# Four of eighteen V products per tile on GpSimd in the channel stage of a four-layer transformer kernel

## The chip, the cores and the metric

The kernel runs on one core of one Trainium2 chip, in one launch. The metric is the device time in microseconds (us); lower is better. The engines are named PE (TensorE), DVE (VectorE), ACT (ScalarE), POOL (GpSimd) and SP (SyncE, which here only issues transfers). Times inside a run are counted from the start of the profiled span. Lnnn is a line of the kernel before, in the text and in its profile.

## The reference, cut to what matters

The batch of 4 sequences of 512 tokens with 128 features goes through four layers, each an attention and a feed-forward part with a layer norm behind each. All is fp32. The change touches the attention of the last layer, which attends between the 64 channels of a head within one token, not between tokens:

```python
# x: (4, 512, 128); H = 16 heads, C = 64 channels
Q = (x @ Wq + bq).reshape(b, s, H, C) / sqrt(C)
K = (x @ Wk + bk).reshape(b, s, H, C)
V = (x @ Wv + bv).reshape(b, s, H, C)
scores = einsum('bshq,bshk->bshqk', Q, K)      # 64 x 64 for every token and head
scores = where(k > q, -inf, scores)
attn = einsum('bshqk,bshk->bshq', softmax(scores), V)
x = layernorm(x + attn.reshape(b, s, H * C) @ Wo + bo)
```

It also moves two weight matrices of earlier layers, the output projections `L1_attn_Wo` and `L2_attn_W_proj` (1024 x 128 each, 512 KB), in SBUF.

## The kernel before, in words

A loop runs over the 4 items of the batch. In each item the stages follow one another: attention and feed-forward of layers 0, 1 and 2, then the channel attention of layer 3 ("the channel stage"), then the feed-forward of layer 3 (eight experts). Each engine has its own instruction list, written out in order by a Python function per engine, and the engines wait on one another through semaphores (`wait_ge`). Nothing is reordered: an instruction that waits holds up all behind it on its engine.

The channel stage takes the 512 tokens of an item as NT = 4 tiles of 128 tokens (one token per partition). For a tile the scores of all 16 heads, causal part only, are cut into NC = 18 chunks of at most 1536 columns: chunks 0 to 5 for the upper half of the queries, 6 to 17 for the lower half without its first 8 queries. A chunk has one to five pieces (blocks of neighbouring keys with the same queries); each piece is one instruction on DVE or POOL. Chunks 0 to 3 have two pieces each, chunks 6 to 14 one piece of 1536 columns. A chunk passes these steps:

- POOL, line L1321: product q*k into one of the five buffers D3 (chunk n uses buffer n mod 5). It waits until the chunk five before has been weighed and its denominator summed.
- DVE, L1366 (`subtract`): subtracts an upper bound of the scores, which `maxima` (L1352 to L1354) has put in PSUM from two scans over the keys (`scan_keys`, L1339).
- ACT, L1297: exponential in place.
- DVE, L1380 (`weigh`): multiplies with V, read from PSUM (`psV`), into one of the two buffers W3.
- PE, L1201 (`sum_chunk`): sums over the keys by transposing matmuls that accumulate in PSUM, once for the denominator (psD, from D3) and once for the numerator (psA, from W3). "den(c)" and "num(c)" are these for chunk c of a tile. The numerator of a chunk is issued one chunk later than its denominator.

The scores of the first 8 queries of the lower half ("own" scores) are made apart, by 128 ACT instructions per tile (L1287), nine or ten behind the exponential of each of the chunks 1 to 14, into the single buffer EA. When all are done, PE sums them (L1210, `sum_own`) in four parts for the denominator at chunks 15 and 16, DVE multiplies them with V (L1386) at chunks 16 and 17, and PE sums them for the numerator at chunk 17 and at chunk 0 of the next tile. Only then may ACT write EA again, at chunk 1 of the next tile.

DVE's list per chunk c is: what is due at c (`maxima` at 0 and 14, `scan_keys` at 12, `finish` at 3 and 8, residual at 7), then subtract(c + 2), then weigh(c). PE projects Q and K of the next tile at chunks 8 to 11 (`fill_qk`, L1172 and L1173: two matmuls and two for the bias), behind num(c - 1), and ACT moves each result to SBUF at chunks 9 to 12 (L1269, L1273), behind the exponential of that chunk. V of a tile is projected in two halves, at chunk 17 of the tile before and at chunk 3.

Weights lie in SBUF for the whole launch, except those of layer 0's feed-forward: they are loaded again by SP at each item's end (L1452), since the channel stage's buffers reach over their place (`LENT` columns behind the shared `arena`). SP then waits for the last norm, writes the output (L1455), and waits for both.

Of the kernel before, what the change touches and what calls it, by code (L numbers as in the profile page):

```python
# [9 lines left out]
ALU = mybir.AluOpType  # L10
# [3 lines left out]
P = 128  # L14
# [43 lines left out]
def transformer(nc, inp, out, last_stage=8):  # L58
    ctx = ExitStack()
    with ctx:  # L60
# [21 lines left out]
        wq1 = sb("wq1", NH * HD)  # L82
        wk1 = sb("wk1", NKV * P)
        wv1 = sb("wv1", NKV * HD)
        wo1 = sb("wo1", NPAIR * P)
        wfc = sb("wfc", HID)
        wpj = sb("wpj", NM * P)
        wa2 = sb("wa2", 3 * NH * HD)
        wo2 = sb("wo2", NPAIR * P)
        ba2 = sb("ba2", 3 * NPAIR)  # L90
        bp2 = sb("bp2", 1)
        bo2 = sb("bo2", 1)
# [21 lines left out]
        stream = [sb(f"stream{j}", SLOT) for j in range(NSLOT)]  # L114


        AR, LENT = 24576, 2 * HID + 2 * NM * HID + NM * P
        arena = sb("arena", AR + LENT)
        top = [AR]

# [8 lines left out]
        w2_0 = take(HID)  # L129
        wh_0 = [take(NM * HID) for _ in range(2)]  # L130
        w3_0 = take(NM * P)

        top[0] = 0

# [51 lines left out]
        D3 = [take(CHUNK) for _ in range(5)]  # L186
        W3 = [take(CHUNK) for _ in range(2)]
        EA = take(HD * NH * OWN)

        top[0] = 0  # L190
        lat = take(HID)
# [16 lines left out]
        def tiles(a, n=P):  # L208
# [9 lines left out]
        ffn0_weights += [(tiles(w, HID), inp[f"L0_ffn_{name}_w"].rearrange("(k p) n -> p k n", p=P))  # L218
                         for w, name in zip(wh_0, ("h1", "h2"))]
        ffn0_weights += [(tiles(w3_0), inp["L0_ffn_w3_w"].rearrange("(k p) n -> p k n", p=P))]  # L220

        consts = sem("consts")
        small_in = sem("small_in")
# [10 lines left out]
        with nc.Block() as block:  # L234
# [15 lines left out]
            @block.scalar  # L250
            def _(act):
                def load(dst, src):
                    act.dma_start(dst, src).then_inc(weights_in, 16)
                    n_w[0] += 16

                load(wqk0[:], inp["L0_attn_QK"])
                load(wvo0[:], inp["L0_attn_VO"])
                for dst, src in ffn0_weights:
                    load(dst, src)
                for j, name in enumerate(("w1", "w2", "h1", "h2")):  # L260
                    load(s_0[:, j * NM:(j + 1) * NM], inp[f"L0_ffn_{name}_s"])
                load(s_0[:, 4 * NM:4 * NM + 1], inp["L0_ffn_w3_s"])
                load(wq1[:], inp["L1_attn_Wq"])
                for half in range(2):
                    load(tiles(wk1[:])[:, :, half * HD:(half + 1) * HD],
                         inp["L1_attn_Wk"].rearrange("d (k c) -> d k c", c=HD))
                load(wv1[:], inp["L1_attn_Wv"])
                load(tiles(wo1[:]), inp["L1_attn_Wo"].rearrange("(k p) n -> p k n", p=P))
                load(wa2[:], inp["L2_attn_W_attn"])
                load(tiles(wo2[:]), inp["L2_attn_W_proj"].rearrange("(k p) n -> p k n", p=P))  # L270
# [137 lines left out]
        def arrived(j):  # L408
# [7 lines left out]
        pr_ = {k: sem(f"prune_{k}") for k in ("s0", "sc", "ff", "bias", "w", "step")}  # L416
        c3 = {k: sem(f"c3_{k}") for k in (
            "d", "e", "w", "den", "num", "attn", "proj", "qk", "qk_sb", "v", "kh", "prod", "chain", "rT",
            "own", "own_den", "own_w", "own_num", "q_ps", "neg")}

        def x_ready(eng, stage):

# [712 lines left out]
        OWN_W = {NC - 2: (0, 1), NC - 1: (2, 3)}  # L1135
        OWN_NUM = {NC - 1: (0, 1), 0: (2, 3)}

        def of_own(o):
            return EA[:, o * PART * NH * OWN:(o + 1) * PART * NH * OWN]

# [73 lines left out]
        def channel_pe(pe):  # L1214
            s = c3
            x_ready(pe, 6)
            for j in range(4):
                fill_qk(pe, 0, j)
            fill_v(pe, 0, 0)
            pe.wait_ge(s["kh"], 2)  # L1220
            idle_work(6, 24)
            for n in range(NALL + 1):
                tt, c = n // NC, n % NC
                if n < NALL:
                    if tt > 0 and c == 0:
                        pe.wait_ge(s["attn"], 2 * tt - 1)
                    if tt > 0 and c == EARLY:
                        pe.wait_ge(s["attn"], 2 * tt)
                    pe.wait_ge(s["e"], n + 1)
                    sum_chunk(psD, D3[n % 5], n).then_inc(s["den"], 1)  # L1230
                if n > 0:
                    pe.wait_ge(s["w"], n)
                    sum_chunk(psA, W3[(n - 1) % 2], n - 1).then_inc(s["num"], 1)
                if n < NALL:
                    for o in OWN_DEN.get(c, ()):
                        pe.wait_ge(s["own"], (tt + 1) * len(own))
                        sum_own(psD, o).then_inc(s["own_den"], 1)
                if n >= NC - 1:
                    of = tt if c == NC - 1 else tt - 1
                    for o in OWN_NUM.get(c, ()):  # L1240
                        pe.wait_ge(s["own_w"], of * PARTS + o + 1)
                        sum_own(psA, o).then_inc(s["own_num"], 1)
                if n == NALL:
                    break
                if c == V1_AT:
                    if tt > 0:
                        pe.wait_ge(s["w"], tt * NC)
                        pe.wait_ge(s["own_w"], tt * PARTS)
                    fill_v(pe, tt, 1)
                if c == PROJ_AT and tt > 0:  # L1250
                    pe.wait_ge(s["d"], tt * NC + EARLY)
                    project_out(pe, tt - 1)
                if c in FILL_AT and tt + 1 < NT:
                    fill_qk(pe, tt + 1, FILL_AT[c])
                if c == V0_AT and tt + 1 < NT:
                    pe.wait_ge(s["w"], tt * NC + LATE)
# [49 lines left out]

        def channel_pool(pool):
            s = c3
            for n in range(NALL):
                tt, c = n // NC, n % NC  # L1310
                ch = chunks[c]
                if c == 0:
                    pool.wait_ge(s["qk_sb"], 4 * tt + 4)
                if n >= 5:
                    pool.wait_ge(s["w"], n - 4)
                    pool.wait_ge(s["den"], n - 4)
                q_half = Q3[tt % 2][:, ch.half * HB_:(ch.half + 1) * HB_]
                for piece in ch.pieces:
                    k, nk, w, at = piece
                    q = queries_on(q_half, ch, piece).rearrange("p k (q h) -> p k q h", h=NH)  # L1320
                    last = nc.gpsimd.tensor_tensor(of_piece(D3[n % 5], piece), q, keys_on(K3[tt % 2], k, nk, w), ALU.mult)  # L1321
                last.then_inc(s["prod"], 1)

        def channel_dve(dve):
            s = c3
# [42 lines left out]

            def weigh(n):
                tt, c = n // NC, n % NC  # L1370
                dve.wait_ge(s["e"], n + 1)
                if c == 0:
                    dve.wait_ge(s["v"], 2 * tt + 1)
                if c == LATE:
                    dve.wait_ge(s["v"], 2 * tt + 2)
                if n >= 2:
                    dve.wait_ge(s["num"], n - 1)
                for piece in chunks[c].pieces:
                    k, nk, w, at = piece
                    last = nc.vector.tensor_tensor(of_piece(W3[n % 2], piece), of_piece(D3[n % 5], piece),  # L1380
                                                   keys_on(psV, k, nk, w), ALU.mult)
                last.then_inc(s["w"], 1)
# [59 lines left out]
        with nc.Fori(0, BATCH) as b:  # L1442
            with nc.Block() as block:
                @block.sync
                def _(sp):
# [2 lines left out]
                    moe_sp(sp, ("L2_ffn_W1", "L2_ffn_W2", "L2_ffn_W3"), 0)  # L1448
                    moe_sp(sp, ("L3_ffn_W1", "L3_ffn_W2"), NE)
                    sp.wait_ge(nrm["xT"], 7)  # L1450
                    for dst, src in ffn0_weights:
                        sp.dma_start(dst, src).then_inc(w0_in, 16)  # L1452
                    sp.wait_ge(nrm["x"], 8 * NT)
                    y = out[bass.ds(b, 1)].rearrange("o (i p) d -> p (o i) d", p=P)
                    sp.dma_start(y, tiles(x[:])).then_inc(y_out, 16)  # L1455
                    sp.wait_ge(y_out, 16)
                    sp.wait_ge(w0_in, 16 * len(ffn0_weights))

                @block.tensor
                def _(pe):  # L1460
# [121 lines left out]
```

## Time and profile before

| what | us |
|---|---|
| median of 3 runs (lowest, highest) | 3764.69 (3761.5, 3766.67) |
| the profiled execution's own time | 3765.0 |
| its span | 3763.4 |
| busy in the span: PE, DVE | 3193.0, 2395.7 |
| busy in the span: ACT, POOL | 1966.7, 1330.0 |
| first item's channel stage, first instruction to the norm's xT | 497 to 890 |

The busy times are over the whole span, and the stages have different limits, so they are to be read stage by stage. "Idle before" an instruction is the time its engine stood still ahead of it, and the arrow names what ended it. Rows of the timeline merge instructions of one line that follow one another: start, time from the first's start to the last's end, engine, line, operation, and the number after x. Since instructions of an engine overlap a little at their ends, the cost of one in a row of several is the distance of two starts.

### The profile page before, as it was taken

What the parts mean: (1) busy time and instruction counts of PE and PEld (TensorE: products, weight loads), DVE (VectorE), ACT (ScalarE), POOL (GpSimd) and SP (SyncE); (2) the same over time, 40 slices, a digit from 0 to 9 for tenths busy, and PEclk for the clock granted to TensorE, in tenths of its full rate; (3) what the DMA queues carried; (4) which work ended last, traced back from release to release, by engine and by line L of the source; (5) the groups of instructions that cost most, each with busy time, mean ns of one, the idle gap of its engine ahead of it and who ended that gap; (6) DMA issues with size and microseconds to landing.
All of it is one profiled execution on the core that took longest, in us unless ns stands there. A gap on an engine that the chain in (4) does not pass through costs nothing. (4 is left out here: it accounts for less than half of the span.)

```text
span 3763.4 us, 52030 instructions
## 1 busy us (share of the span) xinstructions
PE 3193.0 (85%) x19436; PEld 2178.2 (58%) x19436; DVE 2395.7 (64%) x4521; ACT 1966.7 (52%) x4372; POOL 1330.0 (35%) x1068
## 2 busy tenths in 40 slices
PE   4897998888788798888978879888897887988888
PEld 2554557776355546777535554677753555477774
DVE  3357379994246638999415653899931575399983
ACT  1436267773253527777225352877622544277762
POOL 0213056670021307666003120766500312086640
PEclk9998999999899999999989989999998999999999
DMA  3000100000200010000110001000011000100001
GB/s 127 1 1 1 46 14 1 1 1 24 67 1 1 1 53 7 1 1 1 59 32 1 1 1 59 1 1 1 1 59 32 1 1 1 59 1 1 1 1 62
DMA packets 69652, 68.38 MB, mean 18 GB/s; under 512 B 6491, under 2 KB 49907, under 8 KB 69254
## 3 DMA queue, kind: packets, MB, share of 16 engines
q1 hardware_dynamic: 60288, 56.15, 4.8%
q10 hardware_dynamic: 9094, 8.72, 0.7%
q8 instruction: 158, 2.59, 0.3%
q14 instruction: 112, 0.92, 0.1%
HBM read 63.81 MB, written 1.05 MB: 17 GB/s over the span
## 5 line engine op out<-in xcount | busy, mean ns | idle before, releaser
L1321 POOL TENSOR_TENSOR arena<-arena 128x1536 f32<-128x1536 f32 (+9 forms) x480 | 1021.7, 2160 | 415.6 <-DVE arena L1380 327.6
L1201 PE MATMUL psum<-ident,arena 128*128 128x128 f32 (+7 forms) x7168 | 863.8, 278 | 226.5 <-ACT arena L1297 210.1
L1201 PEld LDWEIGHTS psum<-ident,arena 128*128 128x128 f32 (+7 forms) x7168 | 782.8, 136 | 337.2 <-ACT arena L1297 273.6
L1287 ACT ACTIVATE arena<-arena 128x64 f32<-128x64 f32 (+7 forms) x2048 | 714.3, 498 | 140.8 <-PE psum L1210 140.8
L1380 DVE TENSOR_TENSOR arena<-arena,psum 128x1536 f32<-128x1536 f32 (+9 forms) x480 | 495.5, 1068 | 57.4 <-ACT arena L1297 49.7
L1366 DVE TENSOR_TENSOR arena<-arena,psum 128x1536 f32<-128x1536 f32 (+9 forms) x480 | 495.1, 1066 | 8.1 <-POOL arena L1321 6.2
L483 POOL TENSOR_TENSOR rstd<-veps,mhalf 128x4 f32<-128x4 f32 x32 | 32.4, 1012 | 1242.4 <-DVE veps L474 1242.4
L1297 ACT ACTIVATE arena<-arena 128x1536 f32<-128x1536 f32 (+2 forms) x288 | 409.4, 1429 | 117.1 <-DVE arena L1366 116.7
L774 POOL TENSOR_SCALAR arena<-arena 128x512 f32<-128x512 f32 (+3 forms) x512 | 264.5, 532 | 579.9 <-DVE arena L746 579.9
L703 ACT ACTIVATE arena<-arena 128x512 f32<-128x512 f32 (+3 forms) x512 | 282.8, 554 | 267.3 <-DVE arena L741 266.8
L660 PE MATMUL psum<-ident,arena 128*128 128x128 f32 x1280 | 194.8, 297 | 152.9 <-ACT arena L714 91.2
L660 PEld LDWEIGHTS psum<-ident,arena 128*128 128x128 f32 x1280 | 149.9, 151 | 259.2 <-ACT arena L714 140.3
L982 PE MATMUL psum<-arena,stream 128*128 128x512 f32 x512 | 265.7, 601 | 5.0 <-DVE arena L1103 5.0
L999 PE MATMUL psum<-arena,stream 128*128 128x512 f32 x512 | 240.0, 592 | 0.0
L1210 PE MATMUL psum<-ident,arena 128*128 128x128 f32 (+7 forms) x2048 | 234.0, 273 | 0.0
L450 ACT ACTIVATE xT<-psum 128x512 f32<-128x512 f32 x32 | 19.1, 598 | 406.9 <-PE psum L442 406.9
L1099 DVE TENSOR_TENSOR arena<-arena,psum 128x512 f32<-128x512 f32 x128 | 88.0, 688 | 214.2 <-PE psum L999 214.2
L1210 PEld LDWEIGHTS psum<-ident,arena 128*128 128x128 f32 (+7 forms) x2048 | 223.4, 138 | 1.2
L431 PEld LDWEIGHTS psum<-ident 128*128 128x128 f32 x1656 | 205.0, 200 | 26.6 <-issue 20.5
L431 PE MATMUL psum<-ident 128*128 128x128 f32 x1656 | 212.6, 283 | 2.8 <-ACT arena L695 2.8
L1031 ACT ACTIVATE arena<-psum 128x512 f32<-128x512 f32 x128 | 76.6, 598 | 264.6 <-PE psum L999 264.6
L635 PE MATMUL psum<-arena 64*128 64x256 f32 (+3 forms) x1024 | 198.2, 496 | 9.6 <-DVE arena L736 7.7
(209 smaller groups left out, 4105.4 us busy)
## 6 DMA issues: line engine op xcount, KB each, us to landing
stream<-in_L_ffn_W SPq DMA_DIRECT2D x160, 256.0 KB, 3.1
arena<-in_L_ffn_h_w SPq DMA_DIRECT2D x8, 1024.0 KB, 8.0
arena<-in_L_ffn_w_w SPq DMA_DIRECT2D x12, 256.0 KB, 4.5
arena<-in_L_ffn_h_w ACTq DMA_DIRECT2D x2, 1024.0 KB
wa<-in_L_attn_W_attn ACTq DMA_DIRECT2D x1, 1536.0 KB
wq<-in_L_attn_Wq ACTq DMA_DIRECT2D x2, 512.0 KB
wo<-in_L_attn_Wo ACTq DMA_DIRECT2D x2, 512.0 KB
x<-in_L_attn_x SPq DMA_DIRECT2D x4, 256.0 KB, 4.0
```

The source lines that it names most:

```text
L431: nc.tensor.matmul(psum[:, bank, 0:P], ident[:], ident[:], start=True, stop=True)
L660: last = nc.tensor.transpose(GX[:, half, c:c + P], two(PRG[b % 4])[:, half, c:c + P], ident[:])
L703: nc.scalar.activation(pr, pr, ACT.Exp, bias=nb[:, u:u + 1], scale=HD ** -0.5, accum_out=rsum[:, u:u + 1]).then_inc(s["probs"], 1)
L774: nc.gpsimd.tensor_scalar(pr, pr, rinv[:, u:u + 1], 1.0, ALU.mult, ALU.mult).then_inc(s["scaled"], 1)
L982: nc.tensor.matmul(psO, slot[:, 2 * HID + m * P:2 * HID + (m + 1) * P], HR[n % 3], start=n == 0, stop=top2 and n == NE * NM - 1).then_inc( ...
L1201: last = nc.tensor.matmul(ps[ch.half][0:rows, to:to + P], buf[:, c:c + rows], ident[:], start=first, stop=False, is_transpose=True, skip_g ...
L1210: last = nc.tensor.matmul(ps[0][0:rows, 0:P], EA[:, k * NH * OWN:k * NH * OWN + rows], ident[:], start=False, stop=k == HD - 1, is_transpo ...
L1287: nc.scalar.activation(by_key[:, 0:HD - r, j], keys[:, h, 0:HD - r], ACT.Exp, bias=NB[:, j:j + 1], scale=Q3[tt % 2][:, j:j + 1]).then_inc( ...
L1297: nc.scalar.activation(D3[n % 5][:, 0:cols], D3[n % 5][:, 0:cols], ACT.Exp).then_inc(s["e"], 1)
L1321: last = nc.gpsimd.tensor_tensor(of_piece(D3[n % 5], piece), q, keys_on(K3[tt % 2], k, nk, w), ALU.mult)
L1366: last = nc.vector.tensor_tensor(d, d, queries_on(psM[ch.half], ch, piece), ALU.subtract)
L1380: last = nc.vector.tensor_tensor(of_piece(W3[n % 2], piece), of_piece(D3[n % 5], piece), keys_on(psV, k, nk, w), ALU.mult)
```

## The change

Per tile, chunks 1, 3, 7 and 11 are multiplied with V by POOL instead of DVE. POOL cannot take V from PSUM where DVE reads it, so DVE copies the first half of V (512 columns, the channels that these chunks need) to a new SBUF buffer VS at chunk 0 of each tile. POOL writes to one new buffer WP of 1536 columns, and PE's num(c) of these chunks reads WP, waiting on a semaphore `wp` of its own. POOL does the multiplication of chunk n behind the product of chunk n + 3. DVE's two W3 buffers now go round over the 14 chunks that it keeps. To make room for VS and WP the two output projections move to the lent region and are loaded again with the layer 0 weights at each item's end.

```diff
-        wo1 = sb("wo1", NPAIR * P)
-        wo2 = sb("wo2", NPAIR * P)
-        AR, LENT = 24576, 2 * HID + 2 * NM * HID + NM * P
+        AR, LENT = 24576, 2 * HID + 2 * NM * HID + NM * P + 2 * NPAIR * P
+        wo1 = take(NPAIR * P)
+        wo2 = take(NPAIR * P)
+        WP = take(CHUNK)
+        VS = take(NH * HD // 2)
...
+        POOL_W = (1, 3, 7, 11)
+        def on_pool(n):
+            return n % NC in POOL_W
+        def w_before(n):
+            return n // NC * (NC - len(POOL_W)) + sum(c not in POOL_W for c in range(n % NC))
+        def wp_before(n):
+            return n - w_before(n)
+        def weighed(eng, n):
+            if on_pool(n):
+                eng.wait_ge(c3["wp"], wp_before(n) + 1)
+            else:
+                eng.wait_ge(c3["w"], w_before(n) + 1)
+        def weighed_in(n):
+            return WP if on_pool(n) else W3[w_before(n) % 2]
...
         def channel_pe(pe):
                 if n > 0:
-                    pe.wait_ge(s["w"], n)
-                    sum_chunk(psA, W3[(n - 1) % 2], n - 1).then_inc(s["num"], 1)
+                    weighed(pe, n - 1)
+                    sum_chunk(psA, weighed_in(n - 1), n - 1).then_inc(s["num"], 1)
...
         def channel_pool(pool):
+            def weigh_on_pool(n):
+                pool.wait_ge(s["e"], n + 1)
+                pool.wait_ge(s["v_sb"], n // NC + 1)
+                if wp_before(n) > 0:
+                    before = max(m for m in range(n) if on_pool(m))
+                    pool.wait_ge(s["num"], before + 1)
+                for piece in chunks[n % NC].pieces:
+                    k, nk, w, at = piece
+                    last = nc.gpsimd.tensor_tensor(of_piece(WP, piece), of_piece(D3[n % 5], piece), keys_on(VS, k, nk, w), ALU.mult)
+                last.then_inc(s["wp"], 1)
...
                 if n >= 5:
-                    pool.wait_ge(s["w"], n - 4)
+                    weighed(pool, n - 5)
                     pool.wait_ge(s["den"], n - 4)
...
                 last.then_inc(s["prod"], 1)
+                if n >= 3 and on_pool(n - 3):
+                    weigh_on_pool(n - 3)
...
         def channel_dve(dve):
             def weigh(n):
                 tt, c = n // NC, n % NC
-                dve.wait_ge(s["e"], n + 1)
                 if c == 0:
                     dve.wait_ge(s["v"], 2 * tt + 1)
+                    if tt > 0:
+                        dve.wait_ge(s["wp"], wp_before(n))
+                    nc.vector.tensor_copy(VS, psV[:, 0:NH * HD // 2]).then_inc(s["v_sb"], 1)
+                if not on_pool(n):
+                    dve.wait_ge(s["e"], n + 1)
...
-                    for dst, src in ffn0_weights:
+                    for dst, src in lent_weights:
                         sp.dma_start(dst, src).then_inc(w0_in, 16)
```

POOL, first tile of an item, from the last pieces of chunk 5 to chunk 16. Before, L1321 is the product q*k, and the nine of 1536 columns are chunks 6 to 14:

```order
L1321 TENSOR_TENSOR arena<-arena 128x128
L1321 TENSOR_TENSOR arena<-arena 128x64
L1321 TENSOR_TENSOR arena<-arena 128x1536 x9
L1321 TENSOR_TENSOR arena<-arena 128x1280
L1321 TENSOR_TENSOR arena<-arena 128x256
```

In the changed kernel L1361 is that product and L1346 the multiplication with V (832 and 704 columns are the two pieces of chunk 3, the single ones of 1536 columns chunks 7 and 11):

```order
L1361 TENSOR_TENSOR arena<-arena 128x128
L1361 TENSOR_TENSOR arena<-arena 128x64
L1361 TENSOR_TENSOR arena<-arena 128x1536
L1346 TENSOR_TENSOR arena<-arena 128x832
L1346 TENSOR_TENSOR arena<-arena 128x704
L1361 TENSOR_TENSOR arena<-arena 128x1536 x4
L1346 TENSOR_TENSOR arena<-arena 128x1536
L1361 TENSOR_TENSOR arena<-arena 128x1536 x4
L1346 TENSOR_TENSOR arena<-arena 128x1536
L1361 TENSOR_TENSOR arena<-arena 128x1280
L1361 TENSOR_TENSOR arena<-arena 128x256
```

Four instructions on V have come between the products: chunk 3's behind the product of chunk 6, chunk 7's behind that of chunk 10, chunk 11's behind that of chunk 14. Chunk 1's (960 and 576 columns) stand likewise behind the product of chunk 4.

DVE, first tile of an item, chunks 0 to 2. Before, L1366 subtracts and L1380 multiplies with V:

```order
L1380 TENSOR_TENSOR arena<-arena,psum 128x1024
L1380 TENSOR_TENSOR arena<-arena,psum 128x512
L1366 TENSOR_TENSOR arena<-arena,psum 128x832
L1366 TENSOR_TENSOR arena<-arena,psum 128x704
L1380 TENSOR_TENSOR arena<-arena,psum 128x960
L1380 TENSOR_TENSOR arena<-arena,psum 128x576
L1366 TENSOR_TENSOR arena<-arena,psum 128x768
```

In the changed kernel L1417 is the copy of V, L1408 subtracts and L1427 multiplies:

```order
L1417 COPY arena<-psum 128x512
L1427 TENSOR_TENSOR arena<-arena,psum 128x1024
L1427 TENSOR_TENSOR arena<-arena,psum 128x512
L1408 TENSOR_TENSOR arena<-arena,psum 128x832
L1408 TENSOR_TENSOR arena<-arena,psum 128x704
L1408 TENSOR_TENSOR arena<-arena,psum 128x768
```

The copy stands ahead of chunk 0's multiplication, and chunk 1's (960 and 576 columns) is gone. The order of PE's instructions is the same in both kernels; what num(1), num(3), num(7) and num(11) wait for is now POOL's semaphore.

## Rows read from the trace of the kernel before

**Rows 1.** The profile page: busy time of each engine, and POOL's group of products.

```profile
PE 3193.0 (85%) x19436; PEld 2178.2 (58%) x19436; DVE 2395.7 (64%) x4521; ACT 1966.7 (52%) x4372; POOL 1330.0 (35%) x1068
...
L1321 POOL TENSOR_TENSOR arena<-arena 128x1536 f32<-128x1536 f32 (+9 forms) x480 | 1021.7, 2160 | 415.6 <-DVE arena L1380 327.6
```

**Rows 2.** Busy time in stretches of the first item's channel stage.

```profile
core 0: us, PE busy (x) PEld busy (x) DVE busy (x) ACT busy (x) POOL busy (x), PEclk, DMA share, GB/s
497.00:889.97 392.97, 333.94 (x2545) 282.27 (x2543) 355.08 (x325) 283.07 (x611) 256.19 (x121) 0.98 0.00 1
...
609.27:675.10 65.83, 53.87 (x387) 43.72 (x385) 60.92 (x53) 63.66 (x148) 48.96 (x20) 0.97 0.00 1
676.60:703.20 26.60, 26.58 (x229) 24.77 (x230) 26.53 (x26) 5.67 (x5) 16.39 (x12) 1.00 0.01 1
858.25:881.60 23.35, 23.35 (x212) 22.79 (x212) 16.72 (x10) 2.06 (x2) 0.00 (x0) 1.00 0.00 1
```

**Rows 3.** Timeline of ACT, second tile of the first item.

```profile
609.27 3.18 ACT L1287 ACTIVATE arena<-arena 128x64 f32<-128x64 f32 x9 [11.46 <-PE psum L1210]
...
616.66 1.47 ACT L1297 ACTIVATE arena<-arena 128x1536 f32<-128x1536 f32 x1
...
638.38 1.48 ACT L1297 ACTIVATE arena<-arena 128x1536 f32<-128x1536 f32 x1
...
654.64 1.50 ACT L1297 ACTIVATE arena<-arena 128x1536 f32<-128x1536 f32 x1
...
703.47 3.17 ACT L1287 ACTIVATE arena<-arena 128x64 f32<-128x64 f32 x9 [12.28 <-PE psum L1210]
```

**Rows 4.** Timeline of PE, end of that tile and start of the next.

```profile
676.62 3.27 PE L1201 MATMUL psum<-ident,arena 128*128 128x128 f32 x28 [1.82 <-ACT arena L1297]
...
699.70 3.66 PE L1210 MATMUL psum<-ident,arena 128*128 128x128 f32 x32
```

**Rows 5.** Timeline of DVE: chunk 1's multiplication, the scan, the first of `maxima`.

```profile
609.56 1.82 DVE L1380 TENSOR_TENSOR arena<-arena,psum 128x960 f32<-128x960 f32 x2
...
657.85 6.59 DVE L1339 TENSOR_TENSOR_SCAN arena<-first,arena 128x1024 f32<-128x1024 f32 x2
...
671.20 1.05 DVE L1352 TENSOR_TENSOR arena<-psum,arena 128x512 f32<-128x512 f32 x1
```

**Rows 6.** Instructions by form: DVE's copies from PSUM in an earlier stage.

```profile
L757 DVE COPY arena<-psum 128x512 f32<-128x512 f32 x56 | 37.9, 678 | 12.5 <-PE psum L660 12.3
```

**Rows 7.** Timeline of POOL: first tile of the first item, then the second tile.

```profile
504.17 44.89 POOL L1321 TENSOR_TENSOR arena<-arena 128x1024 f32<-128x1024 f32 x23 [13.23 <-ACT arena L1269]
551.09 6.92 POOL L1321 TENSOR_TENSOR arena<-arena 128x1536 f32<-128x1536 f32 x2 [2.04 <-DVE arena L1380]
...
653.66 3.60 POOL L1321 TENSOR_TENSOR arena<-arena 128x1280 f32<-128x1280 f32 x2
658.34 7.18 POOL L1321 TENSOR_TENSOR arena<-arena 128x1024 f32<-128x1024 f32 x2 [1.07 <-PE psum L1201]
```

**Rows 8.** Timeline of PE, first tile, chunk 8: den(8) and num(7), then the fill.

```profile
546.53 2.84 PE L1201 MATMUL psum<-ident,arena 128*128 128x128 f32 x24 [1.86 <-ACT arena L1297]
549.21 1.02 PE L1172 MATMUL psum<-wk,xT 128*128 128x512 f32 x2
550.16 1.12 PE L1173 MATMUL psum<-bqkv,ones 1*128 1x512 f32 x2
```

**Rows 9.** Timeline of ACT, first tile: exponential of chunk 9, then the move.

```profile
549.32 1.50 ACT L1297 ACTIVATE arena<-arena 128x1536 f32<-128x1536 f32 x1
551.32 0.60 ACT L1269 ACTIVATE arena<-psum 128x512 f32<-128x512 f32 x1 [0.49 <-PE psum L1173]
```

**Rows 10.** The last item's end: clock, DMA share and GB/s; then SP's issues.

```profile
3732.00:3736.00 4.00, 1.00 0.98 352
3736.00:3740.00 4.00, 1.00 0.01 3
...
3753.07 0.39 SPq L1455 DMA_DIRECT2D out_x<-x  x1
```

More of the change, by code:

```diff
@@ L220, in transformer @@
         ffn0_weights += [(tiles(w3_0), inp["L0_ffn_w3_w"].rearrange("(k p) n -> p k n", p=P))]
+        out_weights = [(tiles(w), inp[name].rearrange("(k p) n -> p k n", p=P))
+                       for w, name in ((wo1, "L1_attn_Wo"), (wo2, "L2_attn_W_proj"))]
+        lent_weights = ffn0_weights + out_weights
         consts = sem("consts")
@@ L267, in _ @@
                 load(wv1[:], inp["L1_attn_Wv"])
-                load(tiles(wo1[:]), inp["L1_attn_Wo"].rearrange("(k p) n -> p k n", p=P))
+                load(*out_weights[0])
                 load(wa2[:], inp["L2_attn_W_attn"])
-                load(tiles(wo2[:]), inp["L2_attn_W_proj"].rearrange("(k p) n -> p k n", p=P))
+                load(*out_weights[1])
                 load(ba2[:], inp["L2_attn_b_attn"])
@@ L418, in transformer @@
             "d", "e", "w", "den", "num", "attn", "proj", "qk", "qk_sb", "v", "kh", "prod", "chain", "rT",
-            "own", "own_den", "own_w", "own_num", "q_ps", "neg")}
+            "own", "own_den", "own_w", "own_num", "q_ps", "neg", "v_sb", "wp")}
         def x_ready(eng, stage):
@@ L1246, in channel_pe @@
                     if tt > 0:
-                        pe.wait_ge(s["w"], tt * NC)
+                        pe.wait_ge(s["w"], w_before(tt * NC))
                         pe.wait_ge(s["own_w"], tt * PARTS)
@@ L1255, in channel_pe @@
                 if c == V0_AT and tt + 1 < NT:
-                    pe.wait_ge(s["w"], tt * NC + LATE)
+                    pe.wait_ge(s["w"], w_before(tt * NC + LATE))
                     pe.wait_ge(s["own_w"], tt * PARTS + PARTS // 2)
@@ L1370, in weigh @@
                 tt, c = n // NC, n % NC
-                dve.wait_ge(s["e"], n + 1)
                 if c == 0:
                     dve.wait_ge(s["v"], 2 * tt + 1)
[L1374 to L1382, printed above, removed]
+                    if tt > 0:
[3 more added lines that the diff above has]
+                    dve.wait_ge(s["e"], n + 1)
+                    if c == LATE:
+                        dve.wait_ge(s["v"], 2 * tt + 2)
+                    if w_before(n) >= 2:
+                        before = [m for m in range(max(0, n - NC), n) if not on_pool(m)][-2]
+                        dve.wait_ge(s["num"], before + 1)
+                    for piece in chunks[c].pieces:
+                        k, nk, w, at = piece
+                        last = nc.vector.tensor_tensor(of_piece(weighed_in(n), piece), of_piece(D3[n % 5], piece),
+                                                       keys_on(psV, k, nk, w), ALU.mult)
+                    last.then_inc(s["w"], 1)
                 for o in OWN_W.get(c, ()):
@@ L1456, in _ @@
                     sp.wait_ge(y_out, 16)
-                    sp.wait_ge(w0_in, 16 * len(ffn0_weights))
+                    sp.wait_ge(w0_in, 16 * len(lent_weights))
                 @block.tensor
```

## The prediction, made before the changed kernel was run

> **What bounds the kernel now.** I read the page's busy times first [rows 1]. PE leads over the whole span, but the change touches only the channel stage, so I next cut that stage out of the trace. In the first item it takes 393 us, and there DVE is the busiest engine: 355.1 us of 393.0, against 333.9 of PE, 283.1 of ACT and 256.2 of POOL [rows 2]. POOL's longest waits in it are for the very line that is moved, L1380 [rows 1]. By that, DVE looks like the bound. The order of the waits says otherwise.
>
> A tile of the stage is a ring of two stretches. In the first, ACT works almost without a gap: from the first own scores at 609.27 to 675.10 it is busy 63.66 of 65.83 us [rows 2, 3]. What it still waits for there is PE's fills, not DVE. In the second, PE works without a gap: from 676.60 to 703.20 it is busy 26.58 of 26.60 us, from den(15) to the last own numerator [rows 2, 4]. Each is released by the other. PE starts that stretch at 676.62, when ACT's exponential of chunk 15 is done [rows 4]; ACT's own scores of the next tile start at 703.47, released by PE's L1210, after 12.28 us of idle time [rows 3]. Together 65.83 + 26.60 plus about 1.8 us of hand-overs is 94.2 us, the distance from 609.27 to 703.47. The item's last tile ends in the same way, PE busy 23.35 of 23.35 us [rows 2]. DVE fits about 89 us of work per tile (355.1 / 4) beside this ring without holding it up. It is the fullest engine, but not one that the ring waits for.
>
> **The change, part by part.**
>
> *DVE loses work.* Chunk 1's two pieces take 1.82 us [rows 5], chunk 3's are as wide in sum, and chunks 7 and 11 have the same 1536 columns in one piece. Four times about 1.8 us is 7.2 us per tile. The copy of V comes in at 0.68 us, the row of the same form in an earlier stage [rows 6]. Net 6.5 us less per tile, 104 us over 16 tiles. It comes off an engine that neither stretch waits for, so I count it as 0. The price if that is wrong is the first rival.
>
> *POOL gains work.* A product of 1536 columns costs POOL 3.46 us (6.92 for two), one in two pieces 3.60 us [rows 7]. The trace has no multiplication by V on POOL. It has the same columns and operand types as the product, but one operand is read in full where the product repeats it. I take the product's price: 3.60 + 3.60 + 3.46 + 3.46 = 14.1 us per tile. Bounds: DVE's 1.82 us for the same columns below [rows 5]; above, 7.18 us, the dearest chunk of POOL, which ran beside DVE's scan [rows 5, 7].
>
> *First tile of an item: POOL is late.* Here POOL starts with nothing prepared. It runs 23 instructions, the products of chunks 0 to 12, in one piece from 504.17 to 549.06 [rows 7]. The product of chunk 10 thus ends at 549.06 - 6.92 = 542.14. Now the multiplications of chunks 1, 3 and 7 stand ahead of or right behind it, 10.66 us, and no wait of theirs ends later than POOL gets there, so chunk 7 is weighed at 552.80. PE's list has num(7) ahead of the first fill for the next tile, and ACT's list has the move of that fill ahead of nine own scores. num(7) is half of the 24 matmuls whose next instruction starts 2.68 us after them, 1.34 us; the fill lasts from 549.21 to 551.28, 2.07 us [rows 8]. So the fill ends at 552.80 + 1.34 + 2.07 = 556.21, and ACT can move it at 556.25, with the 0.04 us hand-over that it has now. Before, it did at 551.32 [rows 9]. ACT's stretch is 4.93 us longer, and nothing behind it gives this back: the rest of ACT's list is full, and PE's full stretch starts from ACT's end. The other three items show the same pair of rows, POOL's run ending 2.25 to 2.45 us before the move, which gives 4.7 to 4.9 us. Sum: about 19.5 us.
>
> Further down the same tile POOL stays behind. Chunk 15's product comes after the multiplication of chunk 11, and along product 15, subtraction 15, chunk 13, `maxima`, subtraction 16 and chunk 14 DVE comes some 3 us later than before to the end of its part. Since ACT and PE are then 4.93 us late themselves, this costs nothing on top.
>
> *Other tiles.* POOL has caught up at a tile's start, since the ring holds it back while PE finishes the last tile. Chunk 3 is weighed when its exponential is there, at 618.13 [rows 3]: 3.60, then four products of 3.46 and chunk 7's own 3.46 give 639.1. PE needs it after den(8), which waits for the exponential of chunk 8, at 639.86, and takes 1.34: 641.2 [rows 3, 8]. 2.1 us to spare. Chunk 11's exponential ends at 656.14 [rows 3], and DVE's scan, some 4 us earlier now, lies on POOL's multiplication. In the trace a 3.6 us chunk took 7.18 beside a scan, so about 2.5 us of its work needed the 6.1 us that they shared [rows 5, 7]. At that rate chunk 11 is weighed at about 662.3, chunk 15's product ends at 665.9. Behind it on DVE stand two subtractions and two multiplications at 1.75 to 1.8 us and `maxima` at some 2.8 (three instructions, the first 1.05 [rows 5]), so chunk 14 is weighed at about 675.8. PE wants it after den(15), at 676.62 plus 16 of 28 matmuls, 678.4 [rows 4]. 2.6 us to spare. So 0, if POOL's price holds.
>
> The Trainium skill has a rule on that scan (SBUF — State Buffer, "Who interferes with whom"): a DVE instruction with two SBUF inputs contends with GpSimd instructions that read SBUF, one with a single SBUF input does not. It would double the multiplication of chunk 11 and leave chunks 1, 3 and 7 alone, since DVE's neighbours there read one operand from PSUM; the 7.18 us beside 3.60 agree.
>
> *Transfers.* Two more loads of 512 KB per item. The loads there now run at 352 GB/s and are over before 3740; the output is issued at 3753.07 [rows 10]. 1 MB at that rate is 3 us, in a gap of 13. Cover for it is the last two experts and the norm; if it were gone it would cost 3 us per item. Counted as 0.
>
> Sum: 3763.4 + 19.5 = 3782.9 us of span, 3784.5 for the profiled execution. That execution (3765.0) lies 0.3 above the median of 3764.69, so I predict 3784 us, 0.5% slower. What a measurement of this kernel can tell from no change is about 0.2%, 7.5 us.
>
> **Rivals.**
>
> *DVE is the bound after all (faster).* For it: 355 of 393 us busy, and POOL waiting 327.6 us for L1380. Against it: the two full stretches. The price is the net 6.5 us on each of 16 tiles, 104 us: 3661. It decides if ACT's first stretch shortens when DVE is lighter. The Trainium skill has this as its rule of method (Perfetto Trace Analysis, "Identifying the Most-Contended Engine"): the engine with the highest occupancy is the one to relieve first. By the trace's waits it fails here, since the fullest engine is not what ends the ring's waits.
>
> *POOL's lateness is absorbed (no change).* If POOL multiplies at nearly DVE's price, 1.9 us, the three multiplications of the first tile take 5.7 instead of 10.66 us and the move comes at 551.3: 3765. For it: only that POOL's price for this operand pattern is not in the trace. Against: its products show one price per column in all forms.
>
> *POOL is dearer (much slower).* At 1.5 times the product's price the first tile slips by 5.3 us more, 10.2; and in the second and third tile, which also have a fill, chunks 3 and 7 take 3.5 us more where 2.1 are to spare, 1.4 us each. 13.0 us per item, 52 in all: 3817. It decides from a price of about 1.3 times on. At twice the price it would be about 100 us.
>
> **How the numbers follow.** Forecast (first tile slips, the rest hides): 0.6. Dearer POOL or a stall in later tiles that I do not see: 0.15. No change within 0.2%: 0.15. DVE the bound, or some of it: 0.1, most of it below the range. The forecast alone runs from 3773 to 3796 (an item's slip between 2 and 8 us, for a POOL price between 0.75 and 1.25 of the product's). With the no-change case and most of the dear one the range is 3762 to 3812. Slower by over 0.2%: 0.75; within: 0.15; faster: 0.1.
>
> **What would show it.** In each item's first tile POOL should run without a gap for about 55 us, ACT's first move should wait about 5.4 us for PE's fill instead of 0.49, and PE should wait for POOL ahead of num(7). The distance between first own scores of later tiles should stay at 94 us. DVE's busy time should fall by about 104 us, to 2292, and POOL's rise by 226, to 1556. The prediction is wrong if ACT's stretch in later tiles changes, or if PE waits for POOL there.

## The result, and the profile after

| kernel | median us (lowest, highest) | ratio to before, 95% interval |
|---|---|---|
| before, beside it | 3765.68 (3761.5, 3767.25) | |
| changed | 3792.03 (3788.55, 3793.67) | 1.0071 [1.0053, 1.0088] |

The changed kernel is slower by 0.7%, 26 us. 3784 was forecast, in a range of 3762 to 3812.

The page of the changed kernel answers to [rows 1]: busy time of each engine, then the products (L1361, L1321 before), DVE's subtraction (L1408) and multiplication (L1427), and POOL's new multiplication (L1346). The last two columns are busy us with the mean ns of one, and the engine's idle us just before them with what ended it.

```profile
PE 3213.6 (85%) x19436; PEld 2198.4 (58%) x19436; DVE 2280.4 (60%) x4441; ACT 1960.0 (52%) x4372; POOL 1528.7 (40%) x1164
...
L1361 POOL TENSOR_TENSOR arena<-arena 128x1536 f32<-128x1536 f32 (+9 forms) x480 | 975.9, 2075 | 118.1 <-ACT arena L1297 53.7
...
L1427 DVE TENSOR_TENSOR arena<-arena,psum 128x1536 f32<-128x1536 f32 (+13 forms) x384 | 381.0, 1027 | 113.7 <-ACT arena L1325 105.5
...
L1346 POOL TENSOR_TENSOR arena<-arena 128x960 f32<-128x960 f32 (+2 forms) x96 | 249.1, 2612 | 136.1 <-ACT arena L1325 86.2
```

DVE has lost 115 us of work and the kernel is slower. DVE's idle time before its own multiplications that ACT ended has grown from 49.7 us to 105.5.

The ring of a later tile is as it was. These are stretches of the changed kernel's second tile, the answer to [rows 2]: ACT's stretch, then PE's.

```profile
core 0: us, PE busy (x) PEld busy (x) DVE busy (x) ACT busy (x) POOL busy (x), PEclk, DMA share, GB/s
618.62:684.38 65.76, 53.61 (x387) 43.74 (x385) 52.78 (x47) 63.54 (x148) 57.52 (x24) 0.97 0.00 1
685.80:712.40 26.60, 26.60 (x229) 24.78 (x230) 26.53 (x26) 5.51 (x5) 18.12 (x12) 1.00 0.00 1
```

Where before 65.83 and 26.60 us stood, 65.76 and 26.60 stand now. DVE does 8 us less in the first stretch, and ACT's 63.66 are now 63.54.

The first tile is where the time went. POOL's timeline there answers to [rows 7], ACT's to [rows 9], PE's to [rows 8]. The item's stage starts 2.1 us later in this execution (table load of ACT at 513.88 against 511.80).

```profile
506.25 17.98 POOL L1361 TENSOR_TENSOR arena<-arena 128x1024 f32<-128x1024 f32 x11 [13.34 <-ACT arena L1297]
524.18 3.60 POOL L1346 TENSOR_TENSOR arena<-arena 128x960 f32<-128x960 f32 x2
527.72 6.37 POOL L1361 TENSOR_TENSOR arena<-arena 128x384 f32<-128x384 f32 x6
534.03 3.64 POOL L1346 TENSOR_TENSOR arena<-arena 128x832 f32<-128x832 f32 x2
537.59 13.79 POOL L1361 TENSOR_TENSOR arena<-arena 128x1536 f32<-128x1536 f32 x4
551.28 3.49 POOL L1346 TENSOR_TENSOR arena<-arena 128x1536 f32<-128x1536 f32 x1
```

```profile
551.93 1.47 ACT L1325 ACTIVATE arena<-arena 128x1536 f32<-128x1536 f32 x1
560.78 0.60 ACT L1297 ACTIVATE arena<-psum 128x512 f32<-128x512 f32 x1 [7.38 <-PE psum L1201]
```

```profile
548.03 2.84 PE L1229 MATMUL psum<-ident,arena 128*128 128x128 f32 x24 [0.87 <-DVE arena L1427]
554.83 2.82 PE L1229 MATMUL psum<-ident,arena 128*128 128x128 f32 x12 [3.95 <-POOL arena L1346]
557.44 1.92 PE L1200 MATMUL psum<-wk,xT 128*128 128x512 f32 x2
559.28 1.46 PE L1201 MATMUL psum<-bqkv,ones 1*128 1x512 f32 x2
```

POOL runs without a gap to 554.77, PE waits 3.95 us for it, and ACT's wait for the first fill has gone from 0.49 to 7.38 us. num(7) and the fill take 5.9 us where 3.4 were expected. PE's granted clock offers a reason, which e7 below tests (stretches of PE: window, its length, PE's busy time with the number of matmuls, granted clock, DMA):

```profile
548.00:552.00 4.00, 2.84 (x24) 1.00 0.00 0
552.00:555.00 3.00, 0.17 (x1) 0.70 0.00 0
555.00:556.00 1.00, 1.00 (x6) 0.50 0.00 0
```

PE had stood still for 3.95 us; then the clock was 0.5 (1.2 of 2.4 GHz), until about 560. A wait is not all there is to it. In the same tile PE had waited 3.60 us for POOL ahead of num(1), and the 42 matmuls behind that wait ran at 1.0 in 4.80 us; in the second and fourth item the same 42 took 6.47. And the clock fell to 0.5 behind a wait of only 1.17 us too, at 566.60.

A table by tile makes the comparison. Each figure is the distance between two of ACT's rows: table load to the second tile's first own scores, then from tile to tile, then to the norm's xT; sums over the four items.

| kernel | first tiles (4) | later tiles (12) | all |
|---|---|---|---|
| before | 390.7 | 1122.7 | 1513.4 |
| changed | 420.5 | 1117.6 | 1538.0 |

29.8 us lost in the first tiles, 5 us won in the later ones. That is 24.6 us of the 28.3 by which the spans of the two profiled executions differ (3791.7 against 3763.4); the other 3.7 lie outside the rows of this table, 2.1 of them ahead of the first item's channel stage, and their cause stays open.

### The profile page after: what moved, and what is told of

Its sections match the earlier page's. It is cut to its first block and busy times, and to the rows that moved or that the text cites. A ratio compares the mean times of both kernels' runs of the same rounds, so it can differ in the third digit from the quotient of the medians.

```text
span 3791.7 us, 52070 instructions
## 1 busy us (share of the span) xinstructions
PE 3213.6 (85%) x19436; PEld 2198.4 (58%) x19436; DVE 2280.4 (60%) x4441; ACT 1960.0 (52%) x4372; POOL 1528.7 (40%) x1164
## 5 line engine op out<-in xcount | busy, mean ns | idle before, releaser
L1361 POOL TENSOR_TENSOR arena<-arena 128x1536 f32<-128x1536 f32 (+9 forms) x480 | 975.9, 2075 | 118.1 <-ACT arena L1297 53.7
L1229 PEld LDWEIGHTS psum<-ident,arena 128*128 128x128 f32 (+7 forms) x7168 | 797.4, 138 | 339.0 <-ACT arena L1325 242.9
L1408 DVE TENSOR_TENSOR arena<-arena,psum 128x1536 f32<-128x1536 f32 (+9 forms) x480 | 492.5, 1065 | 90.8 <-POOL arena L1361 88.6
L1427 DVE TENSOR_TENSOR arena<-arena,psum 128x1536 f32<-128x1536 f32 (+13 forms) x384 | 381.0, 1027 | 113.7 <-ACT arena L1325 105.5
L1346 POOL TENSOR_TENSOR arena<-arena 128x960 f32<-128x960 f32 (+2 forms) x96 | 249.1, 2612 | 136.1 <-ACT arena L1325 86.2
L1238 PEld LDWEIGHTS psum<-ident,arena 128*128 128x128 f32 (+7 forms) x2048 | 223.4, 138 | 1.2
L436 PEld LDWEIGHTS psum<-ident 128*128 128x128 f32 x1656 | 206.6, 201 | 26.6 <-issue 20.5
L436 PE MATMUL psum<-ident 128*128 128x128 f32 x1656 | 214.1, 284 | 2.7 <-ACT arena L700 2.7
```

The lines of the kernel that those rows point to most:

```text
L436: nc.tensor.matmul(psum[:, bank, 0:P], ident[:], ident[:], start=True, stop=True)
L1229: last = nc.tensor.matmul(ps[ch.half][0:rows, to:to + P], buf[:, c:c + rows], ident[:], start=first, stop=False, is_transpose=True, skip_g ...
L1238: last = nc.tensor.matmul(ps[0][0:rows, 0:P], EA[:, k * NH * OWN:k * NH * OWN + rows], ident[:], start=False, stop=k == HD - 1, is_transpo ...
L1408: last = nc.vector.tensor_tensor(d, d, queries_on(psM[ch.half], ch, piece), ALU.subtract)
L1427: last = nc.vector.tensor_tensor(of_piece(weighed_in(n), piece), of_piece(D3[n % 5], piece), keys_on(psV, k, nk, w), ALU.mult)
```

## The experiments

Each is set against the kernel before on the same chip. The changed kernel has no run of its own beside them, so a difference to its 3792.03 us can be one between chips; the argument rests on the distances between ACT's rows, counted as in the table above.

**Which tiles lose (e1).** POOL weighs nothing in the first tile.

```diff
-            return n % NC in POOL_W
+            return n >= NC and n % NC in POOL_W
```

> The changed kernel, but in the first tile of each item DVE multiplies all chunks with V again; POOL takes its four chunks in tiles 2 to 4 only. Theory A (the ring of ACT's and PE's full stretches sets the time, and the loss is POOL's lateness at num(7) in the first tile): the distance from ACT's table load to the own scores of the second tile falls from 104.7 back to 97.5 us, the later tiles stay where the changed kernel has them, 0.2 to 0.4 us shorter than before, and the time is 3758 to 3765 us, although DVE is relieved in 12 of 16 tiles. Theory B (POOL's work, the loads or the new addresses cost time in every tile): the time stays above 3772. Theory C (DVE is the bound and the first tile only hid it): 12 x 6.5 = 78 us less than before, 3687.

3765.88 us, 1.0003 [0.9994, 1.0012]. First tiles 389.1 us, later 1120.6 (1120.8 in e4, whose DVE has all its work). The whole loss is gone, and 12 tiles with a lighter DVE are worth nothing that can be measured. Theories B and C fall.

**Chunk 7 back on DVE (e3).** Chunks 1, 3 and 11 stay on POOL.

```diff
-        POOL_W = (1, 3, 7, 11)
+        POOL_W = (1, 3, 11)
```

> The changed kernel with chunks 1, 3 and 11 on POOL and chunk 7 back on DVE. Theory A: num(7) waits for DVE as before, POOL is 3.5 us less late, and the first tile's distance is 98 us (0.5 us left at chunk 7's exponential): 3759 to 3767 us. Rival (the loss goes with POOL's total work): three quarters of it stays, about 3785.

3776.17 us, 1.0032 [1.0019, 1.0044]; first tiles 101.3 to 103.7 us instead of 98. About 60% of the loss went: a miss between theory A (3759 to 3767) and its rival (3785). ACT's waits in the first tile name a second path:

```profile
551.39 0.60 ACT L1297 ACTIVATE arena<-psum 128x512 f32<-128x512 f32 x1 [1.52 <-PE psum L1201]
...
560.50 0.60 ACT L1297 ACTIVATE arena<-psum 128x512 f32<-128x512 f32 x1 [3.35 <-PE psum L1201]
```

ACT waits only 1.5 us for the first fill, but 3.4 us for the second. DVE had waited 3.43 us for the product of chunk 7, which POOL made 7 us later than before, and came late to chunk 8's multiplication; num(8) stands ahead of the second fill as num(7) does ahead of the first. PE again stood still (2.55 us) and ran on at half clock (0.52 from 556 to 559). DVE's wait, then PE's:

```profile
537.59 1.75 DVE L1408 TENSOR_TENSOR arena<-arena,psum 128x1536 f32<-128x1536 f32 x1 [3.43 <-POOL arena L1361]
```

```profile
555.35 2.76 PE L1229 MATMUL psum<-ident,arena 128*128 128x128 f32 x12 [2.55 <-DVE arena L1427]
```

POOL's lateness thus reaches PE's list in two ways, and where the first is taken away the second shows.

**Room only (e4).** The two projections lent, nothing on POOL, no copy.

```diff
-        wo1 = sb("wo1", NPAIR * P)
-        wo2 = sb("wo2", NPAIR * P)
+        wo1 = take(NPAIR * P)
+        wo2 = take(NPAIR * P)
...
-                    for dst, src in ffn0_weights:
+                    for dst, src in lent_weights:
```

> The kernel before with only the room lent: the two output projections lie in the lent region and are loaded again each item; no chunk on POOL, no copy of V. Theory A: the loads are hidden, so the time is that of before, 3765, or a few us less if the 14 ns that an own score is shorter in the changed kernel come from the moved addresses (then later tiles are 0.2 to 0.4 us shorter). Theory B (loads cost): 3 us per item more, 3777.

3765.12 us, 0.9999 [0.999, 1.0008]. The loads are hidden. In the changed kernel's last item SP issues the two at 3756.56 and 3758.44, the second in 4.90 us, and the output only at 3781.49. The stage's sum is 1510.0 us, 3.4 less than before (1.5 of it in the first tiles, 1.9 in the later ones), with the own scores at a mean of 483 ns as in the changed kernel (484, before 498). Of the 5 us that the later tiles win, 1.9 thus come with the moved buffers and not from DVE. The rest lies for the most part in the second tiles of the second and fourth item, 92.4 us against 94.0 in the others; in that of the second item the granted clock was 1.00 over the whole tile, in that of the first 0.98.

**Fill ahead of the numerator (e2), and the scan by itself (e6).**

```diff
+                if c in FILL_AT and n < NALL and tt + 1 < NT:
+                    fill_qk(pe, tt + 1, FILL_AT[c])
                 if n > 0:
                     weighed(pe, n - 1)
...
-                if c in FILL_AT and tt + 1 < NT:
-                    fill_qk(pe, tt + 1, FILL_AT[c])
```

> The changed kernel, but PE issues each fill for the next tile ahead of the numerator of the same chunk instead of behind it, so that the fill at chunk 8 does not stand behind num(7), which waits for POOL. Theory A (in-order wait on POOL): ACT's wait for the first fill, 7.4 us in the first tile, goes to under 0.5 us. What is left in that tile is the second chain on POOL (chunk 15's product behind chunk 11's multiplication, some 3 us) and 0.5 us at chunk 7's exponential, so the first tile's distance is about 101 us and the time 3774 to 3780. Theory B (POOL's lateness reaches ACT through DVE's subtractions, not through the fill): no change, 3788 to 3796.

3796.43 us, 1.0084 [1.007, 1.0097]. ACT's first fill came without a wait, as theory A has it, yet the first tile took 107.6 to 109.4 us instead of 101, and the time missed theory A's by 16 us. DVE's timeline shows the cause, beside POOL's:

```profile
562.84 1.75 DVE L1408 TENSOR_TENSOR arena<-arena,psum 128x1536 f32<-128x1536 f32 x1
564.51 16.55 DVE L1381 TENSOR_TENSOR_SCAN arena<-first,arena 128x1024 f32<-128x1024 f32 x2
581.10 1.75 DVE L1408 TENSOR_TENSOR arena<-arena,psum 128x1536 f32<-128x1536 f32 x1
```

```profile
552.45 13.79 POOL L1361 TENSOR_TENSOR arena<-arena 128x1536 f32<-128x1536 f32 x4
566.12 3.53 POOL L1346 TENSOR_TENSOR arena<-arena 128x1536 f32<-128x1536 f32 x1
569.53 7.21 POOL L1361 TENSOR_TENSOR arena<-arena 128x1280 f32<-128x1280 f32 x4
```

The scan stands for 16.55 us, until 4.3 us after POOL's last instruction (569.53 + 7.21 = 576.74). In the changed kernel all its scans take 4.47 us, since POOL happens to wait there for the exponential of chunk 11; before it was 6.59 [rows 5]. There it is POOL that pays. Its multiplication of chunk 11 started 2.1 us before the scan's end (569.92 + 4.47 = 574.39) and took 5.37 us where chunk 7's took 3.49:

```profile
572.27 5.37 POOL L1346 TENSOR_TENSOR arena<-arena 128x1536 f32<-128x1536 f32 x1 [3.87 <-ACT arena L1325]
```

e6 adds to e2 a wait of POOL, ahead of the product of chunk 14, for the end of DVE's scan:

```diff
+                if c == SCAN + 2 and tt + 1 < NT:
+                    pool.wait_ge(s["chain"], 7 * (tt + 1))
```

> The kernel with each fill ahead of the numerator (e2), but POOL starts the product of chunk 14 only when DVE's scan of the next tile's keys is done. Theory A (in e2 the scan in the first tile took 16.55 us because POOL worked without a pause beside it and DVE could not get in; it is 4.47 us with POOL idle): the scan takes 4.5 us in all tiles, the first tile's distance falls from 109 to 102 to 105 us, although POOL's work is started later; 3770 to 3785. Theory B (the scan was long for another reason, or POOL's late start costs as much): 109 us or more stay in the first tile, 3796 or more.

The mechanism was right: 4.47 us for the first tile's scan, and that tile 102.5 to 102.9 us. The time was not: 3798.51 us, 1.0092 [1.0076, 1.0107], since POOL's later start costs the second and third tile 2.4 to 4 us each (93.9 to 95.6, in e2 91.5).

**The clock behind the wait (e5, e7).** Idle matmuls in PE's wait for POOL, 28 and then 17.

```diff
+                if n == 8:
+                    pe.wait_ge(s["d"], EARLY)
+                    idle_work(2, 28)
```

> The changed kernel, but PE makes 28 idle matmuls into a bank that is free there, ahead of its wait for POOL before num(7) in the first tile, instead of standing still for 4 us. Theory A (the first tile's slip of 7.3 us is 4.9 us of POOL's lateness and 2.4 us because num(7) and the fill behind the wait ran at half the granted clock, 5.9 us instead of 3.4): the first tile's distance falls from 104.7 to about 102.3 us and the time by about 10 us, to 3780 to 3784. Theory B (the 2.4 us have another cause, such as a slow semaphore from POOL): no change, 3790 to 3794.

3792.01 us, 1.0071 [1.0057, 1.0085]: theory B's time, but it settles nothing, because the idle matmuls lasted 6.2 us and ended 2.2 behind POOL. num(7) and the fill did run at full clock. So once more with 17 in place of 28:

> As e5, with 17 idle matmuls instead of 28. In e5 the idle matmuls took 6.2 us and ended 2.2 us behind POOL's multiplication of chunk 7, but num(7) and the fill behind them ran at the full clock in 3.4 us. 17 take 3.8 us and end when POOL does. Theory A (half clock behind the wait costs 2.4 us of the first tile's 7.3): first tile's distance 102.0 to 102.5 us, the time 3780 to 3784. Theory B: 104 us or more, 3790 or more.

3780.15 us, 1.0044 [1.0031, 1.0058]. PE's timeline (L436 is the idle work; the trace has two rows for each of the 17):

```profile
551.98 3.96 PE L436 MATMUL psum<-ident 128*128 128x128 f32 x34
556.13 1.53 PE L1229 MATMUL psum<-ident,arena 128*128 128x128 f32 x12 [0.19 <-POOL arena L1349]
557.50 1.02 PE L1200 MATMUL psum<-wk,xT 128*128 128x512 f32 x2
558.45 1.12 PE L1201 MATMUL psum<-bqkv,ones 1*128 1x512 f32 x2
```

3.4 us from num(7) to the end of the fill, and ACT's wait is 4.93 us, not 7.38. First tiles average 102.7 us (101.5 to 103.2) against 105.1 in the changed kernel: 2.4 us each, 9.7 in all, of the 12 us that the time fell.

**Shorten the ring (f1 to f5).** In PE's stretch two of the own numerators stand behind V's fill, den(0) and num(17), which ACT does not wait for. f1 is the kernel before, f2 the changed one, with

```diff
-        OWN_NUM = {NC - 1: (0, 1), 0: (2, 3)}
+        OWN_NUM = {NC - 1: (0, 1, 2, 3)}
```

> The kernel before with one edit: all four own numerators are issued on PE at chunk 17, ahead of V's fill and of den(0) and num(17), instead of two of them behind these. Ring theory: PE's stretch from ACT's last own score to its next first one loses 4.2 us in 12 of 16 tiles, if DVE keeps up: 50 us less, 3715. DVE had 89 to 91 us of work in a ring of 94, so it may keep up only in part: then 30 to 40 us less, 3725 to 3735. Rival (DVE is the bound already): no change, 3765.

> The changed kernel with the same edit as f1. If DVE is what f1's shorter ring runs into, the changed kernel, whose DVE has 6.5 us less per tile, gains more from the edit than the kernel before: 4 us or more in each of 12 tiles, 48 to 55 us less than 3792, 3737 to 3744. If POOL's lateness (2.1 us to spare at num(7) in the later tiles) binds then, less: 3750 to 3765.

f1: 3735.36 us, 0.9926 [0.9911, 0.9941]. f2: 3744.81, 0.9952 [0.9937, 0.9967]. The edit brings 30 us to the kernel before and 47 to the changed one, both at the edge of what I had given. The ring theory holds: an order that takes 4.2 us out of PE's stretch shortens f1's first tiles by 3.6 to 4.5 us and the next two by 0.5 to 2.9. And now DVE counts: the second and third tile take 91.2 to 92.9 us in f1 and 89.6 to 90.5 in f2. The changed kernel only stays behind by its first tiles, 100 us each against 93.4.

f4 is the kernel before with this edit and the fills ahead of the numerators; f3 the same on e1; f5 is f3 with chunk 11 left to DVE.

> e1 (POOL weighs four chunks in tiles 2 to 4 only) with both edits of PE's order: all own numerators at chunk 17, and each fill ahead of the numerator. By the ring the first tile takes 92 to 93.8 us as in f1, the second and third 88 to 89.7 (f2's 89.6 and 90.5, less ACT's waits for fills), the fourth 92.9: 363 to 367 per item against 378.3, 46 to 60 us less than before, 3705 to 3719. Rival (POOL without pauses blocks DVE's scan, as in e2's first tile, once the fills no longer slow ACT): a scan of over 6 us in the second and third tile and a time of 3725 or more.

> The kernel before with both edits of PE's order and no chunk on POOL. If DVE binds a ring shortened in this way, it stays near f1, 3728 to 3735, and f3 beats it by 10 us or more: relieving DVE pays only then. If DVE does not bind: as f3, within 5 us of it.

f4: 3720.71 us, 0.988 [0.9865, 0.9895], the fastest of all, without the change. My expectation for it missed on both sides: it is 15 us ahead of f1 and 45 ahead of f3, which was to beat it. f3: 3765.88, 1.0002 [0.9993, 1.0012]: the rival that I named for it came true. The two scans of the first item's second and third tile:

```profile
649.70 16.55 DVE L1381 TENSOR_TENSOR_SCAN arena<-first,arena 128x1024 f32<-128x1024 f32 x2
745.52 16.57 DVE L1381 TENSOR_TENSOR_SCAN arena<-first,arena 128x1024 f32<-128x1024 f32 x2
```

> As f3, but POOL leaves chunk 11 to DVE (chunks 1, 3 and 7 on POOL, in tiles 2 to 4). In f3 the scan of the second and third tile took 16.55 us, beside a POOL that worked from the product of chunk 12 to that of chunk 16 without a pause, the multiplication of chunk 11 among them. Port theory: with that one gone POOL runs into its wait for DVE soon after the scan begins, and the scan takes 4.5 to 8 us; the second and third tile then take 88.5 to 91 us instead of 95.9, and the time is 3708 to 3722 us, at or below f4's 3721. Rival (the long scan comes from DVE's own state or from PE's new order): 16.5 us stay and the time is 3755 or more.

f5: 3740.53 us, 0.9939 [0.9925, 0.9952]. A miss between both theories; the second and third tile take 92.5 to 94.2 us. The scan takes 10.7 us:

```profile
653.21 10.73 DVE L1381 TENSOR_TENSOR_SCAN arena<-first,arena 128x1024 f32<-128x1024 f32 x2
```

```profile
638.74 20.86 POOL L1361 TENSOR_TENSOR arena<-arena 128x1536 f32<-128x1536 f32 x8
667.47 1.83 POOL L1361 TENSOR_TENSOR arena<-arena 128x768 f32<-128x768 f32 x1 [7.86 <-DVE arena L1427]
```

POOL had one multiplication less to do but still work without a gap until 659.60, 6.4 us into the scan; the scan ended 4.3 us after that. So the scan does wait for POOL's queue, and I misjudged when POOL would pause. In f4 the scans of these tiles take 7.1 us, and there DVE is busy 90.19 of 91.65 us of the second tile, while ACT waits 24.3 us for DVE's subtractions in the second and third tile together: with the ring shortened, DVE is the bound.

## Why the prediction was right, and where it was off

**The bound.** Right. The fullest engine of the stage was not what its ring waited for. DVE lost 115 us of work where 104 were forecast. The terms do not simply add up to that: the multiplications are 114.5 us less, the copy brings 10.9, which is the forecast's 104, and the scans are 25 less because 12 of them now take 4.47 us instead of 6.59. The engine's total counts the overlap of neighbouring instructions once, and with more waits between them there is less overlap. e1 shows that such relief in 12 of 16 tiles is worth nothing. The rule of the Trainium skill that I set against it (Perfetto Trace Analysis, "Identifying the Most-Contended Engine"), to relieve the engine of the highest occupancy first, fails in this trace; it holds in the later tiles of f1 and f2, where the ring has come down to DVE's own work and a lighter DVE makes 17 us.

**POOL's price.** Right. Chunk 7's multiplication took 3.49 us against 3.46, the two-piece chunks 3.60 and 3.64 against 3.60. The rival of a dearer POOL and that of a cheap one both fall by it. Chunk 11's took 5.4 us beside the scan, as the prediction had it in kind (about 6.2), and cost nothing. POOL's busy time rose by 199 us and not by 226: the multiplications cost 249, but the products that used to run beside the scan are 46 less.

**The first tile.** The mechanism was right, and the sum of POOL's run too: forecast 552.80, measured 554.77 with a stage that began 2.08 us later; from there POOL went on without a gap to 568.40, 62 us in one piece where I had said 55. Mis-sized was the term behind it. I took num(7) and the fill at 1.34 + 2.07 = 3.4 us from a row in which PE had not stood still. With 3.95 us of waiting ahead of them they took 5.9. So the slip was 7.2 to 8.0 us instead of 4.9, 29.8 us instead of 19.5 over the items. e7 shows that the clock is what lies between: with it at 1.0 the first tiles are 9.7 us shorter in sum. A term that the sum left out is POOL's lateness by way of DVE, 0.50 us of ACT's waiting ahead of chunk 7's exponential. That 3792 still lies within the 3773 to 3796 of the forecast itself is in part luck, for that width was drawn for POOL's price and not for PE's clock.

**Later tiles.** Forecast as unchanged; they are 5 us shorter in sum, 1.9 of it by the moved room alone (e4). The two margins that I had worked out, 2.1 us at num(7) and 2.6 at chunk 14, held: with the 9.35 us taken off by which the tile starts later than in [rows 3], chunk 7 was weighed at 638.9 (639.1 forecast) and chunk 14 at 675.4 (675.8 forecast), and PE never waits for POOL in a later tile.

**Transfers.** Right, hidden (e4). I took 1 MB at 352 GB/s, 3 us; its issue alone took SP 6.7 us. The gap had room for that.

**What I did not see.** DVE's lateness as a second path from POOL to PE (e3), and that a scan can be held up by all that POOL has ready (e2, f3, f5). In the changed kernel the first shows with 0.50 us only and the second not at all, by the accident that its other delays were longer. Left open is when a scan gets in. Taken one by one, the scan's two instructions say this much. In e2, f3 and f5, where POOL was already working without a gap, the first took 14.37, 14.37 and 8.55 us and the second 2.26. In the kernel before and in e3, where POOL stood still as the first began, the first took 2.28 and the second 4.38 and 5.49: it waited for one instruction of POOL and came ahead of the next. In f4 the first got in between two of POOL's instructions that follow without a gap (2.81 us), as it did not in e2; no run sets the two apart.

## What to carry to other kernels

Find the chain that closes on itself from tile to tile and ask which stretches of it are full, before work is taken off the busiest engine; here an order of PE's list gave 44 us (f4) and four multiplications moved to another engine cost 26. An instruction list is only as early as its latest wait: before work is moved to a slower engine, follow it in the tile in which that engine starts with nothing prepared. And when PE is made to wait, price what stands behind the wait at the lower clock as well as at the full one; here it came out at either.

## What the runs showed of the hardware that I had not expected

- DVE's scan (two instructions, both inputs in SBUF) takes 4.47 us alone and 16.55 us beside a POOL that works on without a pause; in e2, f3 and f5 it ended 4.3 us after POOL's last instruction. The Trainium skill (SBUF — State Buffer, "Who interferes with whom") says that a DVE instruction with two SBUF inputs contends with a GpSimd instruction that reads SBUF, and that the ports they share are an exclusive lock. The traces agree, and show in addition that the scan let five further instructions of POOL start ahead of it in e2.
- A wait of 3.95 us on PE was followed by a granted clock of 0.5 for about 5 us, which cost 2.5 us in that place; 17 idle matmuls in the wait kept num(7) and the fill at full speed, 3.4 us (e7). A wait of 3.60 us in the same tile was not followed by the lower clock, and one of 1.17 us was.
- ACT's own scores fell from a mean of 498 ns to 483 when only the place of buffers in SBUF had changed (e4). The cause stays open.
